# Graph attention kernel: the value product in whole rows of four heads, pair copies alternating between ScalarE and VectorE

## The chip, the core and the metric

The kernel runs on one core of a Trainium2 chip. The metric is the device time of the whole program in microseconds, lower is better. Before the change it is 734.52 us, the median of three runs (733.99 to 735.31).

## The reference, cut to what matters

Sixteen graphs of 512 nodes and 128 features pass through two layers. The first (a norm, a linear map and eight Euler steps of a graph diffusion) is not touched by the change. The second is an attention with four heads of 32 features over each graph, masked by the adjacency:

```python
h = relu(layernorm(x))
qkv = (h @ W).reshape(B, 512, 3, 4, 32).transpose(2, 0, 3, 1, 4)
q, k, v = qkv
scores = einsum('bhid,bhjd->bhij', q, k) / sqrt(32) + mask
attn = softmax(scores, axis=-1)
out = einsum('bhij,bhjd->bhid', attn, v)
x = x + out.transpose(0, 2, 1, 3).reshape(B, 512, 128)
```

All of it is in fp32. The change concerns the last product, `attn` times `v`, and the copies that feed it.

## The kernel before, in words

The kernel has three blocks: a set-up, the diffusion (`ode_block`) and `attention_block` (from line 1107). The second writes q, k, v and the residual of each graph to HBM; the attention reads them back, one graph ("batch") after another.

A batch is 16 score tiles of 128 queries by 512 keys, one for each block of queries and each head. Tile n is block n // 4, head n % 4. Each engine has its own program of a batch, written as a loop over n, and semaphores tie them together. For tile n:

- TensorE (line 1334) multiplies q by k into one of three PSUM banks `ps_s`. It waits until VectorE has emptied the bank, and at n = 0 until the eight q/k loads of this batch have landed.
- VectorE (line 1292) adds the mask, writes the tile to `s_ring` and keeps the row extreme in `low`.
- ScalarE (line 1269) takes the exponential in place and sums it into `lsum`.
- TensorE (line 1321) transposes the tile, four turns later (`LAG = 4`), into half of a two-bank tile `ps_t`. Two tiles are a pair p = 0 to 7; pair p fills `ps_t[p % 2]`, so its transposes wait for the copy of pair p - 2.
- VectorE (line 1286) or ScalarE (line 1260) copies a whole pair, 128 x 1024, to `p_t`. Which engine, is given by `ACT_PAIRS`; where in that engine's order, by `COPY_BEFORE`: pair p is copied before score tile `COPY_BEFORE[p]` of the same batch, and a value of 16 or more means before tile value - 16 of the next batch.

The value product (line 1349) of a batch runs inside the next batch's turns. It has 16 matmuls, k = 0 to 15: row j = k // 4 is a block of 128 keys, hh = k % 4 the head. A head's result takes 32 of the 128 columns of the array and 32 partitions of one bank `ps_o`; the four rows j accumulate. `PV_AT` says behind which turn's transposes how many of them are issued. The first one waits for the last pair copies of both engines, for v and for the bank. Each matmul is fp32 and appears as two instructions in the trace. After turn 13's group ScalarE copies the bank to `o_t` (line 1264), in turn 15 TensorE transposes it back (line 1356), VectorE divides by the sums after score tile 15 (lines 1298 and 1302), and GpSimd adds the residual (line 1246).

SyncE issues all DMAs on one queue, in this order in each batch: v (line 1204, when the value product is done), the residual x1 (line 1206, when GpSimd's add is done), the store of the result (line 1217), then the eight loads of q and k (line 1103), 256 KB each, for the batch behind the one that TensorE has just begun, into the buffers that the last batch has left.

The order of the work is written out by hand in these constants:

```python
ACT_PAIRS = [1, 2, 5, 7]
COPY_BEFORE = [7, 7, 8, 12, 14, 15, 18, 18]
PV_AT = {5: 1, 6: 4, 7: 2, 11: 4, 13: 5}
OCOPY_AT, OT_AT, FIN_AT = 13, 15, 15
```

Batches 1 to 14 are run by a hardware loop whose body holds two batches; batch 0, batch 15 and a last pass without score tiles stand by themselves.

Of the kernel before, what the change touches and what calls it, by code (L numbers as in the profile page):

```python
# [33 lines left out]
HEADS = 4  # L34
HD = D // HEADS
T = N // 128
# [14 lines left out]
def wait(eng, sem, value):  # L51

    if isinstance(value, int) and value <= 0:
        return
    eng.wait_ge(sem, value)  # L55
# [1051 lines left out]
def attention_block(nc, ctx, x1_dram, qk_dram, v_dram, out, keep):  # L1107
# [8 lines left out]
    PAIRS = TILES // 2  # L1116
    RING = 8
    LAG = 4
    ACT_PAIRS = [1, 2, 5, 7]
    DVE_PAIRS = [p for p in range(PAIRS) if p not in ACT_PAIRS]  # L1120

    COPY_BEFORE = [7, 7, 8, 12, 14, 15, 18, 18]


    PV_AT = {5: 1, 6: 4, 7: 2, 11: 4, 13: 5}
    OCOPY_AT, OT_AT, FIN_AT = 13, 15, 15
    assert sum(PV_AT.values()) == HEADS * T
    PV_RANGE = [(sum(PV_AT.get(i, 0) for i in range(n)), sum(PV_AT.get(i, 0) for i in range(n + 1))) for n in range(TILES)]

    S_BANKS = 3  # L1130
# [45 lines left out]
    def copied(p, b):  # L1176

        if p in ACT_PAIRS:
            return t_act, len(ACT_PAIRS) * b + ACT_PAIRS.index(p) + 1
        return t_dve, len(DVE_PAIRS) * b + DVE_PAIRS.index(p) + 1  # L1180

    def pairs_before(n, mine):

        return [(p, COPY_BEFORE[p] // TILES) for p in mine if COPY_BEFORE[p] % TILES == n]

    def copy_pair(eng, p, b, par):
        wait(eng, t_mm, TILES * b + 2 * p + 2)
        if p in (ACT_PAIRS[0], DVE_PAIRS[0]):
            wait(eng, pv_mm, CREDIT + b - 1)
# [62 lines left out]
    def _(act):  # L1252
        def batch(b, par, tiles=TILES):
            first = isinstance(b, int) and b == 0
            for n in range(TILES):
                for p, back in pairs_before(n, ACT_PAIRS):
                    if (first and back) or not (tiles or back):
# [53 lines left out]
    def _(pe):  # L1311
# [13 lines left out]
        def batch(b, par, tiles=TILES):  # L1325
            first = isinstance(b, int) and b == 0
            c, cp = b - 1, 1 - par
            for n in range(TILES):
# [11 lines left out]
                for k in range(*PV_RANGE[n]) if not first else ():  # L1340

                    j, hh = divmod(k, HEADS)
                    if k == 0:
                        for p in (ACT_PAIRS[-1], DVE_PAIRS[-1]):
                            wait(pe, *copied(p, c))
# [19 lines left out]
def graph_block(nc, x, adj, alpha, w, d, fcw, fcb, wqkv, out):  # L1365
    x1_dram = nc.dram_tensor("x1_dram", [B, 128, T, D], F32, kind="Internal").ap()
    qk_dram = nc.dram_tensor("qk_dram", [B, 128, 4, N], F32, kind="Internal").ap()
    v_dram = nc.dram_tensor("v_dram", [B, 128, N], F32, kind="Internal").ap()
    keep = {}
    with ExitStack() as outer:  # L1370
        keep["ident"] = outer.enter_context(nc.sbuf_tensor("ident", [128, 128], F32))
        keep["pH"] = [outer.enter_context(nc.sbuf_tensor(f"pH{k}", [128, T, N], F32R)) for k in range(3)]
        keep["pL"] = [outer.enter_context(nc.sbuf_tensor(f"pL{k}", [128, T, N], F32R)) for k in range(3)]


        assert HEADS == T
        keep["q_st"], keep["k_st"] = keep["pH"][0::2], keep["pL"][0::2]
        for name in ("adj_in", "mask_done", "tail_out"):
            keep[name] = outer.enter_context(nc.semaphore("att_" + name))
        keep["qk_in"] = [outer.enter_context(nc.semaphore(f"qk_in{i}")) for i in range(2)]  # L1380
        with ExitStack() as kept:
            def sb(name, shape, dt=F32R):
                return kept.enter_context(nc.sbuf_tensor(name, shape, dt))
            keep["rH"], keep["rL"] = sb("rH", [128, 3, 3 * D]), sb("rL", [128, 3, 3 * D])
            keep["wH"], keep["wL"] = sb("wH", [128, 3 * D]), sb("wL", [128, 3 * D])
            keep["g"] = sb("g", [128, T, 3 * D], F32)
            ln = FirstNorm(sb, lambda name: kept.enter_context(nc.semaphore(name)))
            with ExitStack() as ctx:
                setup_block(nc, ctx, x, adj, alpha, w, d, fcw, fcb, wqkv, keep, ln)
            with ExitStack() as ctx:  # L1390
                ode_block(nc, ctx, x, adj, x1_dram, qk_dram, v_dram, keep, ln)
        with ExitStack() as ctx:  # L1392
            attention_block(nc, ctx, x1_dram, qk_dram, v_dram, out, keep)
# [20 lines left out]
```

## Time and profile before

| | |
|---|---|
| median of three runs | 734.52 us (733.99 to 735.31) |
| span of the profiled execution | 730.3 us |
| mean granted TensorE clock | 0.982 |
| TensorE matmul busy | 692.7 us, 95% |
| VectorE busy | 486.1 us, 67% |
| ScalarE busy | 400.9 us, 55% |
| GpSimd busy | 121.2 us, 17% |
| value product, line 1349 | 512 instructions of 603 ns, 95.6 us |
| score matmuls, line 1334 | 256 of 495 ns, 126.0 us |
| transposes, line 1321 | 1024 of 275 ns, 155.7 us |
| VectorE pair copy, line 1286 | 64 of 1220 ns |
| ScalarE pair copy, line 1260 | 64 of 1014 ns |

The span is the time between the first and the last instruction of one execution under the profiler; the device time of an execution is longer by what lies around it, 4.2 us between this span and the median. Busy times count overlapping matmuls once, and a matmul's duration includes the part in which the next one already runs. The attention begins at about 413 us; the shares of the whole span mix it with the two blocks before it.

### The profile page before, as it was taken

What the parts mean: (1) busy time and instruction counts of PE and PEld (TensorE: products, weight loads), DVE (VectorE), ACT (ScalarE), POOL (GpSimd) and SP (SyncE); (2) the same over time, 40 slices, a digit from 0 to 9 for tenths busy, and PEclk for the clock granted to TensorE, in tenths of its full rate; (3) what the DMA queues carried; (4) which work ended last, traced back from release to release, by engine and by line L of the source; (5) the groups of instructions that cost most, each with busy time, mean ns of one, the idle gap of its engine ahead of it and who ended that gap; (6) DMA issues with size and microseconds to landing.
All of it is one profiled execution on the core that took longest, in us unless ns stands there. A gap on an engine that the chain in (4) does not pass through costs nothing. (4 is left out here: it accounts for less than half of the span.)

```text
span 730.3 us, 12946 instructions
## 1 busy us (share of the span) xinstructions
PE 692.7 (95%) x3801; PEld 517.3 (71%) x3801; DVE 486.1 (67%) x1272; ACT 400.9 (55%) x860; POOL 121.2 (17%) x100
## 2 busy tenths in 40 slices
PE   7999999998999989999998779999999999999996
PEld 5768987898888978899887655565655555566553
DVE  6753552578337873466346578888888888888883
ACT  3442231233522444222334678888888888888883
POOL 4110343032401233012315000000000000000001
PEclk8999999999999999999998999999999999999999
DMA  3001110311342124400449892666676766766620
GB/s 104 30 0 44 30 44 0 101 31 44 145 167 78 57 80 162 132 15 16 158 175 256 287 213 74 152 139 150 155 158 158 158 148 154 158 157 152 153 57 29
DMA packets 49807, 82.52 MB, mean 113 GB/s; under 512 B 5232, under 2 KB 13808, under 8 KB 49648
## 3 DMA queue, kind: packets, MB, share of 16 engines
q1 hardware_dynamic: 49344, 82.07, 42.5%
q8 instruction: 16, 0.26, 0.2%
q14 instruction: 15, 0.12, 0.1%
q10 hardware_dynamic: 432, 0.07, 0.1%
HBM read 52.76 MB, written 29.36 MB: 112 GB/s over the span
## 5 line engine op out<-in xcount | busy, mean ns | idle before, releaser
L1292 DVE CUSTOM_DVE_ANT_0 s_ring<-ps_s,pL 128x512 f32<-128x512 f32 x256 | 169.0, 688 | 55.0 <-PE ps_s L1334 53.1
L1269 ACT ACTIVATE s_ring<-s_ring,low 128x512 f32<-128x512 f32 x256 | 182.2, 713 | 16.3 <-DVE low L1292 14.8
L1321 PE MATMUL ps_t<-ident,s_ring 128*128 128x128 f32 x1024 | 155.7, 275 | 9.6 <-DVE p_t L1286 9.0
L1321 PEld LDWEIGHTS ps_t<-ident,s_ring 128*128 128x128 f32 x1024 | 127.0, 141 | 31.5 <-DVE p_t L1286 11.6
L1334 PE MATMUL ps_s<-pL,pH 128*128 128x512 f32 x256 | 126.0, 495 | 6.9 <-DMA pL<-qk_dram 3.7
L1334 PEld LDWEIGHTS ps_s<-pL,pH 128*128 128x128 f32 x256 | 48.9, 192 | 75.5 <-DVE low L1292 56.6
L1349 PE MATMUL ps_o<-p_t,v_sb 128*32 128x512 f32 x512 | 95.6, 603 | 1.1 <-ACT p_t L1260 1.1
L1286 DVE COPY p_t<-ps_t 128x1024 f32<-128x1024 f32 x64 | 78.1, 1220 | 0.0
L1260 ACT ACTIVATE p_t<-ps_t 128x1024 f32<-128x1024 f32 x64 | 64.9, 1014 | 21.3 <-PE ps_t L1321 21.3
L1246 POOL TENSOR_TENSOR o_n<-o_n,x 128x512 f32<-128x512 f32 x16 | 20.6, 1285 | 311.4 <-DVE o_n L1302 311.4
L94 PE MATMUL ps_v<-rH,ut_h 128*128 128x384 f32 x192 | 65.1, 339 | 4.6 <-DVE v L927 4.6
L96 PE MATMUL ps_v<-rH,ut_l 128*128 128x384 f32 x192 | 64.5, 336 | 0.0
L95 PE MATMUL ps_v<-rL,ut_h 128*128 128x384 f32 x192 | 64.5, 336 | 0.0
L768 ACT ACTIVATE ut_h<-ps_u 128x512 fp32r<-128x512 f32 x44 | 26.1, 593 | 65.3 <-PE ps_u L96 43.4
L869 DVE TENSOR_TENSOR ut_l<-ps_u,ut_h 128x512 fp32r<-128x512 f32 x44 | 30.3, 688 | 36.2 <-ACT ut_h L768 36.1
L927 DVE TENSOR_TENSOR v<-ps_v,g 128x384 f32<-128x384 f32 x64 | 35.5, 555 | 26.7 <-PE ps_v L96 25.7
L733 POOL TENSOR_TENSOR v_l<-v,v_h 128x512 fp32r<-128x512 f32 x16 | 21.0, 1313 | 176.9 <-ACT v_h L821 176.9
L1269 ACT ACTIVATION_READ_ACCUMULATOR s_ring<-s_ring,low 128x1 f32 x256 | 48.3, 188 | 0.0
L94 PE MATMUL ps_u<-pH,u_h 128*128 128x512 f32 x112 | 45.8, 409 | 0.0
L96 PE MATMUL ps_u<-pH,u_l 128*128 128x512 f32 x112 | 44.3, 395 | 0.0
L95 PE MATMUL ps_u<-pL,u_h 128*128 128x512 f32 x112 | 44.1, 394 | 0.0
L94 PEld LDWEIGHTS ps_v<-rH,ut_h 128*128 128x128 f32 x192 | 36.1, 188 | 6.0 <-DVE v L927 5.6
(201 smaller groups left out, 1087.3 us busy)
## 6 DMA issues: line engine op xcount, KB each, us to landing
pH<-qk_dram SPq DMA_DIRECT2D x64, 256.0 KB, 7.6
pL<-qk_dram SPq DMA_DIRECT2D x64, 256.0 KB, 8.4
qk_dram<-qk SPq DMA_DIRECT2D x12, 512.0 KB, 3.3
x_ln<-in_x SPq DMA_DIRECT2D x16, 256.0 KB, 3.3
x_res<-in_x SPq DMA_DIRECT2D x16, 256.0 KB, 2.6
x_dram<-v SPq DMA_DIRECT2D x16, 256.0 KB, 3.1
v_sb<-v_dram SPq DMA_DIRECT2D x16, 256.0 KB, 2.7
x<-x_dram SPq DMA_DIRECT2D x16, 256.0 KB, 2.9
```

The source lines that it names most:

```text
L94: eng.matmul(psum, lh, rh, start=(first and n == 0), stop=False)
L95: eng.matmul(psum, lh, rl, start=False, stop=False)
L96: mm = eng.matmul(psum, ll, rh, start=False, stop=(last and n == len(pairs) - 1))
L869: dve.tensor_tensor(ut_l[b % 2][:, k, :], u_bank(b, k)[:, :], ut_h[b % 2][:, k, :].bitcast(F32), ALU.subtract).then_inc(ul_done, 1)
L927: dve.tensor_tensor(v[:, t, b, :], ps_v[t % 2][:, 0:3 * D], keep["g"][:, t, :], ALU.add).then_inc(v_add, 1)
L1260: act.activation(dst, src, ACT.Copy).then_inc(t_act, 1)
L1269: act.activation(s_ring[:, n % RING, :], s_ring[:, n % RING, :], ACT.Exp, bias=low[:, n:n + 1], scale=-1.0, accum_out=lsum[par][:, n:n + 1 ...
L1286: dve.tensor_copy(dst, src).then_inc(t_dve, 1)
L1292: dve.tensor_tensor_reduce(s_ring[:, n % RING, :], ps_s[S_BANK[n]][:, :], mask[:, n // HEADS, :], -SCALE, 3.0e38, ALU.add, ALU.min, low[:, ...
L1321: mm = pe.transpose(ps_t[p % 2][:, n % 2, j * 128:(j + 1) * 128], s_ring[:, n % RING, j * 128:(j + 1) * 128], ident[:, :])
L1334: pe.matmul(ps_s[S_BANK[n]][:, :], q_st[par][:, h, it * 128:(it + 1) * 128], k_st[par][:, h, :], start=True, stop=True).then_inc(s_mm, 1)
L1349: mm = pe.matmul(ps_o[cols, :], v_sb[cp][:, j, cols], p_t[cp][:, hh, j, :], start=(j == 0), stop=(j == T - 1), tile_position=(0, HD * hh))
```

## The change

Three tables of the attention are altered and an assertion is tightened. The value product is issued behind turns 5, 9 and 13, four, four and eight matmuls, each a whole number of rows of four heads. Pair 2 passes from ScalarE to VectorE and pair 3 from VectorE to ScalarE, so that odd pairs are ScalarE's and even ones VectorE's. Six of the eight copies are placed at another tile in their engine's order: pair 0 before tile 6 (was 7), pair 2 before 10 (was 8), pair 3 before 13 (was 12), pair 5 before tile 0 of the next batch (was 15), pairs 6 and 7 before its tile 3 (was 2). Nothing else differs.

```diff
-    ACT_PAIRS = [1, 2, 5, 7]
+    ACT_PAIRS = [1, 3, 5, 7]
     DVE_PAIRS = [p for p in range(PAIRS) if p not in ACT_PAIRS]
 
-    COPY_BEFORE = [7, 7, 8, 12, 14, 15, 18, 18]
+    COPY_BEFORE = [6, 7, 10, 13, 14, 16, 19, 19]
 
-    PV_AT = {5: 1, 6: 4, 7: 2, 11: 4, 13: 5}
+    PV_AT = {5: 4, 9: 4, 13: 8}
     OCOPY_AT, OT_AT, FIN_AT = 13, 15, 15
-    assert sum(PV_AT.values()) == HEADS * T
+    assert sum(PV_AT.values()) == HEADS * T and all(n % HEADS == 0 for n in PV_AT.values())
```

## Rows read from the trace of the kernel before

**Rows 1.** Windows, one batch: length, busy us (instructions) by engine, clock, DMA share, GB/s.
```profile
528.70:547.90 19.20, 18.62 (x118) 11.23 (x117) 15.92 (x41) 16.11 (x38) 1.49 (x2) 1.00 0.68 150
```

**Rows 2.** Chain that ended last, in order of time: start us, us, what.
```profile
529.93 0.66 PE ps_t L1321 x4
...
547.93 1.15 DVE p_t L1286
549.12 0.66 PE ps_t L1321 x4
```

**Rows 3.** Timeline of VectorE: start us, us, engine, line, operation.
```profile
527.44 0.68 DVE L1292 CUSTOM_DVE_ANT_0 s_ring<-ps_s,pL 128x512 f32<-128x512 f32 x1
...
546.62 0.69 DVE L1292 CUSTOM_DVE_ANT_0 s_ring<-ps_s,pL 128x512 f32<-128x512 f32 x1
...
547.24 0.69 DVE L1292 CUSTOM_DVE_ANT_0 s_ring<-ps_s,pL 128x512 f32<-128x512 f32 x1
...
547.85 1.22 DVE L1286 COPY p_t<-ps_t 128x1024 f32<-128x1024 f32 x1
```

**Rows 4.** Timeline of TensorE, one batch, turn 0 to the next turn 0.
```profile
526.15 0.48 PE L1334 MATMUL ps_s<-pL,pH 128*128 128x512 f32 x1
...
530.54 0.50 PE L1334 MATMUL ps_s<-pL,pH 128*128 128x512 f32 x1
...
531.40 1.05 PE L1349 MATMUL ps_o<-p_t,v_sb 128*32 128x512 f32 x2
532.38 0.50 PE L1334 MATMUL ps_s<-pL,pH 128*128 128x512 f32 x1
...
533.25 1.06 PE L1349 MATMUL ps_o<-p_t,v_sb 128*32 128x512 f32 x8
...
536.10 0.50 PE L1334 MATMUL ps_s<-pL,pH 128*128 128x512 f32 x1
...
536.79 0.48 PE L1334 MATMUL ps_s<-pL,pH 128*128 128x512 f32 x1
...
537.46 0.48 PE L1334 MATMUL ps_s<-pL,pH 128*128 128x512 f32 x1
...
540.66 0.48 PE L1334 MATMUL ps_s<-pL,pH 128*128 128x512 f32 x1
...
543.34 0.50 PE L1334 MATMUL ps_s<-pL,pH 128*128 128x512 f32 x1
...
545.14 0.48 PE L1334 MATMUL ps_s<-pL,pH 128*128 128x512 f32 x1
```

**Rows 5.** Timeline of ScalarE, the copy of pair 7.
```profile
529.59 1.00 ACT L1260 ACTIVATE p_t<-ps_t 128x1024 f32<-128x1024 f32 x1
```

**Rows 6.** Timeline of SyncE's DMA issues: x1 and last q/k load of two batches.
```profile
509.83 0.35 SPq L1206 DMA_DIRECT2D x<-x_dram  x1
...
515.35 0.65 SPq L1103 DMA_DIRECT2D pL<-qk_dram  x1
...
529.00 0.35 SPq L1206 DMA_DIRECT2D x<-x_dram  x1
...
533.80 0.54 SPq L1103 DMA_DIRECT2D pL<-qk_dram  x1
```

**Rows 7.** DMA issues around 515.35 and 533.80: queue, count, KB, us to landing.
```profile
pL<-qk_dram SPq DMA_DIRECT2D x1, 256.0 KB, 10.3
...
pL<-qk_dram SPq DMA_DIRECT2D x1, 256.0 KB, 10.0
```

**Rows 8.** Timeline of SyncE's DMA issues at the start of the attention.
```profile
419.63 0.34 SPq L1103 DMA_DIRECT2D pL<-qk_dram  x1
420.03 0.63 SPq L1204 DMA_DIRECT2D v_sb<-v_dram  x1
```

**Rows 9.** DMA issues around 419.63 and 420.03, us to landing.
```profile
pL<-qk_dram SPq DMA_DIRECT2D x1, 256.0 KB, 10.4
...
v_sb<-v_dram SPq DMA_DIRECT2D x1, 256.0 KB, 10.9
```

## The prediction

> **What bounds the kernel now.** I went from the page to the windows, then to the chain of waits, then to the timelines of TensorE, VectorE, ScalarE and SyncE over one batch of the attention. The change touches only the attention's loop, whose batches 1 to 15 repeat one pattern. In one such batch TensorE is busy 18.62 of 19.20 us, VectorE 15.92, ScalarE 16.11, at full granted clock (1.00, the 2.4 GHz level) [rows 1]. So no batch can go below about 16.1 us by the busy times of the other two engines, and TensorE is what fills it now. The chain of waits, though, leaves TensorE at one place in each batch: VectorE's pair copy (line 1286), then four transposes that take 0.66 us instead of their usual share, and on [rows 2]. From those transposes to the next ones like them it is 529.93 to 549.12, 19.19 us; the score matmul of turn 0 to that of the next batch is 526.15 to 545.14, 18.99 us [rows 4]. Batches alternate between the two, since the loop's body holds two batches; the mean is 19.09.
>
> I number a batch's turns by the score tile n, 0 to 15. A turn without value product takes 0.69 us right behind a group (536.10 to 536.79) and 0.67 otherwise (536.79 to 537.46) [rows 4]; I take 0.67.
>
> **Part 1, the value product regrouped.** Turn 5 issues one matmul (two instructions) and lasts 530.54 to 532.38 = 1.84; turn 6 issues four (eight instructions) and turn 7 two, and together they last 532.38 to 536.10 = 3.72, 1.86 each [rows 4]. One matmul costs as much as four: the four heads use different 32 columns of the array and run side by side. Every group of up to one of each head costs 1.86 - 0.67 = 1.19 (turn 5: 1.17). Turn 13 issues five, so two on one head's columns, and lasts 540.66 to 543.34 = 2.68, or 2.01 over an empty turn [rows 4]. The trace holds no group of eight between score matmuls. Its lower bound is that same 2.01, since it also has two on each head's columns; its upper bound is two separate groups of four, 2.38. I take 2.03, near the five, because the second row is issued behind the first with no score tile between.
> Before: 1.17 + 1.19 + 1.19 + 1.18 (turn 11, four, as turn 6) + 2.01 = 6.74. After: turns 5, 9, 13 give 1.17 + 1.19 + 2.03 = 4.39. TensorE issues 2.35 us less per batch. Between two bounds for the eight this is 2.0 to 2.37.
>
> **Part 2, which engine copies, and when.** Pair copies are p = 0 to 7; TensorE transposes pair p in turns 2p+4 and 2p+5 (6 and 7 in turns 0 to 3 of the next batch), and the transposes of pair p wait for the copy of pair p-2. Pair 2 goes from ScalarE to VectorE, pair 3 the other way, so each engine keeps four. The edit that costs is pair 6: VectorE did it before score tile 2 of the next batch and now does it before tile 3. Now: score tile 0 starts at 546.62, tile 1 at 547.24, the copy at 547.85, and the transposes of turn 4 start at 549.12 [rows 2, 3]. One VectorE tile takes 547.24 to 547.85 = 0.61 [rows 3]. TensorE reached turn 4 before that (the chain runs through the copy), so nothing hides the 0.61: they start 0.61 later, and everything behind them on TensorE's queue (score tile 5, the value product) waits with them. Lower bound 0, if the copy were not the last to come; upper bound 1.22, if the tile and its successor both fell in front. I take 0.61, the row it is made of.
>
> A rule to weigh. The rows say that VectorE's order, not TensorE's work, sets this stretch, and I take off 0.61 of the 2.35. The Trainium skill, page TensorEngine Tiling (Array Packing), PSUM Bottleneck, warns that packing the array speeds up TensorE but not the copies out of PSUM, which may then become the limit. Without that effect the sum would be 2.35 per batch, with it 1.74.
>
> **The other moves, at nothing, and their cover.** I followed one batch with the starts of the rows, score tile 13 at 0, each operation as soon as its engine and its inputs allow. Turns 14, 15, 0' start at 2.70, 3.37 and 4.48; pair 6 is copied at 7.8, turn 4's transposes start at 9.1, turn 5 at 9.7, turn 13 again at 17.4. (a) Pair 7 on ScalarE goes behind exp 2 instead of before it. Now it starts at 529.59, lasts 1.00, and the first value matmul, which waits for it, starts at 531.40: 0.8 us to spare [rows 4, 5]. ScalarE's step is 0.71 later, TensorE's turn 5 is 0.61 later, so about 0.7 stays. (b) Pair 5 goes behind exp 15 and ends near 6.6 while turn 2's transposes could start at 6.2; this 0.4 us stall, plus a restart, is hidden by the wait for pair 6 at 9.1. If that cover went, it would cost 0.7. (c) Pairs 0 (before tile 6), 2 (VectorE, before tile 10, done near 16.1 against a need at 17.1) and 3 (ScalarE, before exp 13, done 0.4 before turn 14 needs it) fall in VectorE's and ScalarE's free time. If (c) lost its 0.4, the stall would be the excess. (d) No DMA is added or moved, but SyncE's waits are: the x1 load, the store and the eight q/k loads follow the add on GpSimd, which follows score tile 15, at the same distance.
>
> **Part 3, the q/k loads.** They must land before score tile 0 of the next batch. The x1 load is issued at 529.00, the last q/k load at 533.80 and lands 10.0 later, at 543.8; the deadline is 545.14: 1.34 to spare. In the batch before: 515.35 + 10.3 = 525.65 against 526.15, 0.50 to spare [rows 4, 6, 7]. A late score tile 0 is also absorbed until VectorE would start it: it starts 0.69 after TensorE's at the earliest, and now starts at 546.62 and 527.44, 0.79 and 0.60 beyond that [rows 3, 4]. The spare time is 2.1 and 1.1. A batch 1.74 shorter leaves 0.4 and -0.6. Since the stall also delays the next chain of loads, half of the 0.6 or so stays, in every other batch: about 0.2 per pair after the scatter of the landings, 1.5 us in all. Bounds: 0 and 7 x 0.6 = 4.
>
> **Sum.** Batches 1 to 15: 15 x (2.35 - 0.61) = 26.1 us off, 1.5 back, 24.6. Batch 0 has no value product and the next one waits for its loads; the last product (all 16 matmuls without score tiles between) stays one block. From the span of the profiled execution, 730.3, to 705.7. The median of the runs, 734.5, lies 4.2 above that span, the time around it: 734.5 - 24.6 = **709.9**, say 710.
>
> **Rivals.**
> A. The copy of pair 6 costs nothing, all 2.35 arrive: 15 x 2.35 = 35 less, 700. For: VectorE idles elsewhere. Against: the chain goes through this very copy in every batch [rows 2]. Chance 0.08.
> B. The q/k loads become the bound. For: the spare time is used up by the sum itself. Each us that the landing comes later costs about 0.5 per batch (a load issued after one batch is needed two starts later). One us more gives 717, two 724. Against: the load of v is now issued while q/k packets are still in flight, but it need not slow them: at the start, v issued at 420.03 landed after 10.9, at 430.9, behind q/k issued at 419.63 that took 10.4, to 430.0 [rows 8, 9]. Chance 0.17.
> C. Slower than before. The copy of pair 7 on ScalarE comes so late that the first value matmul waits in TensorE's queue, with score tile 6 and all behind it. Its place is turn 5; it decides from 0.7 (the spare time) + 1.74 = 2.4 us of lateness on; at 3 us, 15 x 0.6 = 9 more, 743. For: pair 5 and pair 7 both moved behind one more exp. Against: ScalarE has 3 us free per batch [rows 1], and the exps before it have no other late input. Chance 0.04.
> D. The change does not shorten the groups: a row of four takes longer after other work than turn 6 shows. Then no change, 734. Turn 6 is measured, so 0.03.
> My forecast keeps 0.68.
>
> **Numbers.** A measurement of this kernel can tell about 0.2%, 1.5 us. Range 703 to 719: below, the eight and the loads at nothing and part of A; above, the lighter half of B. Faster 0.93, same 0.03, slower 0.04.
>
> **What would show it.** Right: value product in groups of 8, 8 and 16 instructions, turns 5 and 9 near 1.86, turn 13 near 2.70; transposes of turn 4 released by VectorE's copy, with 0.6 us more wait than now; period near 17.4; score tile 0 now waiting for a DMA by up to 0.9 us in some batches. Wrong: score tile 0 waiting over 1 us in all batches (B); first value matmul released by ScalarE (C); turn 4 without a wait (A); turn 2 or turn 14 on the chain (my free moves).

## The result and the profile after

The changed kernel takes 712.58 us (707.21 to 714.85, four runs) against 734.91 of the kernel before on the same chips: ratio 0.9686, 95% interval 0.9655 to 0.9717, 22.3 us less. A second set of six runs gave 712.27 and 0.9706 (0.9675 to 0.9738). The forecast was 710.0, range 703 to 719.

The profiled execution took 707.21 with a span of 705.4, so 1.8 us lie around the span; it was the quickest of its four. The prediction had put 4.2 there for the kernel before. Every run on record of either kernel is 1.8 or 1.9 longer than its span, so the span of 730.3 belongs to an execution of about 732.1, quicker than all the runs of its median, and the other 2.4 are scatter. The forecast doesn't suffer, since the same amount is taken off both. Medians are compared with medians below, and periods with periods.

The page of the changed kernel, engines and costliest groups:

```profile
PE 655.7 (93%) x3801; PEld 511.2 (72%) x3801; DVE 488.7 (69%) x1272; ACT 398.8 (57%) x860; POOL 121.2 (17%) x100
...
L1321 PE MATMUL ps_t<-ident,s_ring 128*128 128x128 f32 x1024 | 155.4, 275 | 17.4 <-DVE p_t L1286 11.9
...
L1334 PE MATMUL ps_s<-pL,pH 128*128 128x512 f32 x256 | 125.1, 491 | 10.6 <-DMA pL<-qk_dram 7.1
...
L1349 PE MATMUL ps_o<-p_t,v_sb 128*32 128x512 f32 x512 | 64.5, 601 | 1.1 <-ACT p_t L1260 1.1
```

The value product has the same 512 instructions of the same length (601 ns, 603 before) but keeps TensorE busy 64.5 us where it was 95.6: more of them run side by side. TensorE is busy 37 us less in all, and the runs got only 22 us faster. The third column says where part of the rest went: the score matmuls wait 7.1 us for a DMA, eight times, where before it was 3.7, once, in batch 1.

The timeline of TensorE, from one batch's turn 0 to the next, and the later turns 0 (columns: start us, us, instruction, and in brackets the idle time before it with what ended it):

```profile
499.75 0.50 PE L1334 MATMUL ps_s<-pL,pH 128*128 128x512 f32 x1 [1.02 <-DMA pL<-qk_dram]
...
502.45 0.48 PE L1334 MATMUL ps_s<-pL,pH 128*128 128x512 f32 x1
503.75 0.65 PE L1321 MATMUL ps_t<-ident,s_ring 128*128 128x128 f32 x4 [0.82 <-DVE p_t L1286]
504.16 0.48 PE L1334 MATMUL ps_s<-pL,pH 128*128 128x512 f32 x1
...
505.01 1.07 PE L1349 MATMUL ps_o<-p_t,v_sb 128*32 128x512 f32 x8
506.00 0.50 PE L1334 MATMUL ps_s<-pL,pH 128*128 128x512 f32 x1
...
511.92 0.48 PE L1334 MATMUL ps_s<-pL,pH 128*128 128x512 f32 x1
...
512.76 1.92 PE L1349 MATMUL ps_o<-p_t,v_sb 128*32 128x512 f32 x16
514.62 0.50 PE L1334 MATMUL ps_s<-pL,pH 128*128 128x512 f32 x1
...
516.48 0.50 PE L1334 MATMUL ps_s<-pL,pH 128*128 128x512 f32 x1
...
533.49 0.49 PE L1334 MATMUL ps_s<-pL,pH 128*128 128x512 f32 x1
```

Against [rows 4]: turn 5 has four matmuls and lasts 504.16 to 506.00 = 1.84, as with one. Turn 13 has eight and lasts 511.92 to 514.62 = 2.70, against 2.68 with five. Turn 4's transposes still wait for VectorE's copy, 0.82 us here, but the score matmul behind them starts 0.41 later (503.75 to 504.16), where it was 0.61 before ([rows 2, 4], 529.93 to 530.54).

The DMA wait of 1.02 is not in every batch. From the turn 0 behind it to the next, which does not wait, it is 16.73 us (499.75 to 516.48); then 17.01, and the next 18.64 (533.49 to 552.13) with a wait of 1.16. Over 13 periods (first turn 0 446.52, last 674.25) the mean is 17.52, before 19.08. A second profiled execution of the changed kernel, 712.22 us and so near the median, has 17.64 over the same 13 (448.27 to 677.58). The chain of waits says what that long batch hung on: SyncE's last q/k issue, and its landing.

```profile
540.20 0.81 SPq L1103
...
541.10 0.65 SPq L1103
...
541.84 10.17 DMA pL<-qk_dram
...
552.13 0.49 PE ps_s L1334
```

That load is no slower than its like in [rows 6, 7]. From the x1 load to the landing of the last q/k load the changed kernel takes 15.2 us on average over 13 batches, and the kernel before 15.1. What changed is when it is needed.

### The profile page after: what moved, and what is told of

It is laid out like the page before. It is cut to its first block, busy times and chain, and to the rows that moved or that the text cites. A ratio compares the mean times of both kernels' runs of the same rounds, so it can differ in the third digit from the quotient of the medians.

```text
span 705.4 us, 12953 instructions
## 1 busy us (share of the span) xinstructions
PE 655.7 (93%) x3801; PEld 511.2 (72%) x3801; DVE 488.7 (69%) x1272; ACT 398.8 (57%) x860; POOL 121.2 (17%) x100
## 4 chain that ended last, share of the span: by engine, by line
PE 34%; DMA 11%; DVE 6%; issue 5%; SPq 4%; POOL 1%; ACT 1%; POOLq 0%; DVEq 0%; ACTq 0%
DMA pL<-qk_dram 10%; PE ps_t L1321 7%; PE ps_s L1334 5%; PE ps_o L1349 4%; SPq L1103 3%; PE ps_z L1015 2%; PE ps_z L1011 2%; PE ps_z L1010 2%; PE ps_u L94 2%; PE ps_u L96 1%; PE ps_u L95 1%; PE ps_v L94 1%; PE ps_v L96 1%; PE ps_v L95 1%; DVE p_t L1286 1%
## 5 line engine op out<-in xcount | busy, mean ns | idle before, releaser
L1321 PE MATMUL ps_t<-ident,s_ring 128*128 128x128 f32 x1024 | 155.4, 275 | 17.4 <-DVE p_t L1286 11.9
L1349 PE MATMUL ps_o<-p_t,v_sb 128*32 128x512 f32 x512 | 64.5, 601 | 1.1 <-ACT p_t L1260 1.1
L95 PE MATMUL ps_v<-rL,ut_h 128*128 128x384 f32 x192 | 64.5, 336 | 0.0
L768 ACT ACTIVATE ut_h<-ps_u 128x512 fp32r<-128x512 f32 x44 | 26.1, 594 | 65.4 <-PE ps_u L96 43.4
```

What stands on the lines that cost most here:

```text
L95: eng.matmul(psum, lh, rl, start=False, stop=False)
L1321: mm = pe.transpose(ps_t[p % 2][:, n % 2, j * 128:(j + 1) * 128], s_ring[:, n % RING, j * 128:(j + 1) * 128], ident[:, :])
L1349: mm = pe.matmul(ps_o[cols, :], v_sb[cp][:, j, cols], p_t[cp][:, hh, j, :], start=(j == 0), stop=(j == T - 1), tile_position=(0, HD * hh))
```

## Experiments

All were compared with the kernel before on the same chip. There were three of them, on which the kernel before took 734.34 (A), 735.48 (B) and 734.65 (C); where two runs come from different chips, a difference of medians is good to about 1 us, and the ratios are the better guide. Medians in us:

| run | chip | median (runs) | ratio, 95% interval |
|---|---|---|---|
| changed kernel, two sets | -, A | 712.58 (4), 712.27 (6) | 0.9686 (0.9655 to 0.9717), 0.9706 (0.9675 to 0.9738) |
| tables only | B | 741.93 (6) | 1.0097 (1.0069 to 1.0125) |
| groups only | B | 717.53 (6) | 0.9754 (0.9724 to 0.9783) |
| changed, early q/k | B | 707.74 (6) | 0.9615 (0.9588 to 0.9642) |
| changed, late q/k | A | 715.49 (5) | 0.9741 (0.9715 to 0.9767) |
| before, early q/k | A | 734.30 (12) | 1.0000 (0.9978 to 1.0023) |
| before, late q/k | A | 735.24 (12) | 1.0014 (0.9996 to 1.0032) |
| changed, pair 6 first | B | 717.15 (5) | 0.9761 (0.9734 to 0.9789) |
| the same, early q/k | C | 717.19 (6) | 0.9754 (0.9722 to 0.9787) |
| groups, old tables, pair 0 moved | C | 709.62 (6) | 0.9662 (0.9637 to 0.9686) |
| the same, early q/k | C | 705.72 (6) | 0.9605 (0.9575 to 0.9636) |
| early q/k, pairs 5 to 7 at old places | C | 698.16 (6) | 0.9507 (0.9476 to 0.9538) |

**The two halves of the change.** First the tables without the groups:

```diff
-    PV_AT = {5: 4, 9: 4, 13: 8}
+    PV_AT = {5: 1, 6: 4, 7: 2, 11: 4, 13: 5}
```

> The new copy tables with the old groups of the value product (1, 4, 2, 4, 5). Theory: pair 6's copy one score tile later on VectorE puts 0.61 us per batch on the chain, 15 x 0.61 = 9 us slower than before, ratio 1.012. Rival: the tables are free by themselves, within 0.2% of before.

Measured 6.5 us slower than before. The timeline of TensorE in that run:

```profile
508.83 0.48 PE L1334 MATMUL ps_s<-pL,pH 128*128 128x512 f32 x1
...
512.13 0.47 PE L1334 MATMUL ps_s<-pL,pH 128*128 128x512 f32 x1
513.41 0.66 PE L1321 MATMUL ps_t<-ident,s_ring 128*128 128x128 f32 x4 [0.81 <-DVE p_t L1286]
513.83 0.48 PE L1334 MATMUL ps_s<-pL,pH 128*128 128x512 f32 x1
...
528.42 0.48 PE L1334 MATMUL ps_s<-pL,pH 128*128 128x512 f32 x1
```

The direction is the theory's, its size a third smaller. Turn 4's transposes start 4.58 after turn 0 where it was 3.98 in the same half of the loop (545.14 to 549.12, [rows 2, 4]), so the 0.61 is there. But the next score matmul follows after 0.42 instead of 0.61. It waits for tile 2 to leave its PSUM bank, and VectorE now takes tile 2 ahead of the copy. Before, VectorE's tile 2 ended at 549.66, and score tile 5 began 0.07 later:

```profile
548.98 0.68 DVE L1292 CUSTOM_DVE_ANT_0 s_ring<-ps_s,pL 128x512 f32<-128x512 f32 x1
```

The batches take 19.37 and 19.59, the mean is 19.48 against 19.08: 0.40 per batch, 15 x 0.40 = 6.0.

Then the groups without the tables:

```diff
-    ACT_PAIRS = [1, 3, 5, 7]
+    ACT_PAIRS = [1, 2, 5, 7]
-    COPY_BEFORE = [6, 7, 10, 13, 14, 16, 19, 19]
+    COPY_BEFORE = [7, 7, 8, 12, 14, 15, 18, 18]
```

> The new groups (4, 4, 8) with the old tables. Theory: TensorE's 2.35 us per batch come off, but the q/k loads then end last in most batches (period 17.1 where the engines alone would give 16.8), so 15 x 2.0 = 30 off, near 705, and less than the changed kernel's 712.6 by 4 to 8. Rival: the old tables collide with the new groups (pair 2 on ScalarE before tile 8, pair 3 on VectorE before tile 12), and it is slower than the changed kernel, 715 or more.

The rival was right: 717.5, 5 us slower than the changed kernel (3.5 to 5 by the ratios). The timelines of TensorE and of VectorE in two batches of it show a second wait:

```profile
529.21 0.47 PE L1334 MATMUL ps_s<-pL,pH 128*128 128x512 f32 x1
530.51 0.66 PE L1321 MATMUL ps_t<-ident,s_ring 128*128 128x128 f32 x4 [0.83 <-DVE p_t L1286]
```

```profile
546.54 0.69 DVE L1292 CUSTOM_DVE_ANT_0 s_ring<-ps_s,pL 128x512 f32<-128x512 f32 x1 [0.86 <-PE ps_s L1334]
...
547.16 1.22 DVE L1286 COPY p_t<-ps_t 128x1024 f32<-128x1024 f32 x1
```

Turn 8's transposes wait 0.83 us for pair 0. VectorE sat idle for 0.86 with that copy next but one in its order: score tile 6 stood in front, and tile 6 comes only after turn 5's value product. Before, turns 6 and 7 carried value product too and hid this. So the collision is real, but in this run it shows at pair 0, not at pairs 2 and 3 as the rival had it: turn 12's transposes start 0.32 behind their score matmul here, without a wait. That one entry, by itself, on top of the groups:

```diff
     ACT_PAIRS = [1, 2, 5, 7]
-    COPY_BEFORE = [7, 7, 8, 12, 14, 15, 18, 18]
+    COPY_BEFORE = [6, 7, 8, 12, 14, 15, 18, 18]
```

> New groups, old tables, with only pair 0 moved from tile 7 to tile 6. In the run with all old tables (717.5) turn 8's transposes waited 0.8 us for VectorE's copy of pair 0, which stood behind score tile 6, itself behind the four matmuls of turn 5. Theory: this one entry is what the new groups need of the tables; the wait goes, 1.1 us per batch less where the q/k loads allow it: 708 to 712. Rival: several entries are needed, it stays above 715.

709.6: 7.9 us less than with all old tables by the medians, 6.8 by the ratios. That the 3 us to the changed kernel are a gain is not shown, since the intervals overlap. The groups need pair 0 moved; the other changes to the tables, taken together and with the loads where they are, bring nothing measurable on top. The trace has turn 8 without a wait, and another one in its place:

```profile
516.69 0.47 PE L1334 MATMUL ps_s<-pL,pH 128*128 128x512 f32 x1
517.30 0.65 PE L1321 MATMUL ps_t<-ident,s_ring 128*128 128x128 f32 x4
```

This is turn 12, with 0.61 where 0.32 is usual, and so in every batch. The late copy of pair 0 had hidden it; what it is shows below, where the rival's pair 2 comes back.

**Is it the q/k loads?** SyncE issues the eight loads ahead of x1 and the store, in the changed kernel and in the one before:

```diff
         def batch(b, par):
...
-            if not last:
-                load(b + 1, 1 - par)
-            if not first:
-                store(b - 1, 1 - par)
+            if not (const and b == B - 1):
+                load_q(b + 1, 1 - par)
+            if not (const and b == 0):
+                load_x(b, par)
+            if not (const and b < 2):
+                store(b - 2, par)
+            if not (const and b == B - 1):
+                load_v(b + 1, 1 - par)
```

> The changed kernel with SyncE's order altered: the eight q/k loads go ahead of the residual's load and of the store, so they are issued some 4 us earlier in each batch. Theory: the changed kernel's unprofiled runs lose to late q/k loads; with the loads early score tile 0 waits for no DMA, the period is 17.3 to 17.4, the time 703 to 706, and the runs lie within 3 us of each other. Rival: the 4 to 5 us between the changed kernel's median and its fastest run come from elsewhere, and it stays at 711 to 713 with the same scatter.

> The kernel before with the q/k loads ahead of the residual's load and the store. Theory: with a period of 19.1 the loads land 1.1 to 2.1 us before they are needed, so earlier loads bring nothing: within 0.3% of before. Rival: earlier loads help by something else than the wait at score tile 0 (a shorter first batch, less contention), and bring the 5 us that they brought in the changed kernel.

The functions `load_q`, `load_x` and `load_v` are the old `load` in three pieces; they and the first and last batches, written out by themselves, are left out here.

And the same loads held back, in both:

```diff
-                wait(sp, s_mm, CREDIT + TILES * (b - 1))
+                wait(sp, s_mm, CREDIT + TILES * (b - 1) + 6)
```

> The changed kernel with the q/k loads held back until score tile 5 of the batch is done, some 0.6 to 0.9 us later than now. Theory: the loads end last, and each us of lateness costs about half a us per batch: 14 x 0.5 x 0.75 = 5 us more than the changed kernel, near 718. Rival: their landing is hidden, 712 to 713.

> The kernel before with the same hold until score tile 5. Theory: the spare time of 1.1 to 2.1 us covers it, within 0.3% of before. Rival: 5 us slower, as in the changed kernel.

> The changed kernel itself, as the control for the three others of this group. 711 to 713.

Early loads take 4.5 to 4.8 us off the changed kernel (5.2 to 6.7 by the ratios, whose intervals don't touch) and nothing off the kernel before; late loads add 3.2 to the changed one, and to the kernel before 0.9, inside its interval. The 3.2 alone would not be proof, since the intervals of the two ratios overlap; the waits below bear it out. The signs fit the theory; early landed at 707.7, above the 703 to 706 expected, and late cost less than the 5 worked out. With early loads the waits list shows no DMA wait of TensorE from batch 2 on, and turn 0 comes at

```profile
502.37 0.48 PE L1349 MATMUL ps_s<-pL,pH 128*128 128x512 f32 x1
...
519.61 0.48 PE L1349 MATMUL ps_s<-pL,pH 128*128 128x512 f32 x1
...
536.66 0.48 PE L1349 MATMUL ps_s<-pL,pH 128*128 128x512 f32 x1
```

17.24 and 17.05, mean 17.15, a little under the 17.3 to 17.4 expected (the longer program moves the line numbers by 15). That is 0.37 under the changed kernel's 17.52 and 0.50 under the 17.64 of its second profiled execution; over 13 periods 4.9 and 6.5 us, about what the medians say. With late loads every turn 0 from batch 2 on waits, and the mean period is 17.83:

```profile
PE ps_s L1334 <- DMA pL<-qk_dram: 12.8, 14, 1.1
```

The theory said more than that: that the changed kernel's runs scatter because of the loads. This is mostly not so. With early loads the runs still lie within 4.2 us, the changed kernel's within 5.7 in its second set and 7.6 in its first. And of the 5.0 us between the spans of its two profiled executions (705.4 and 710.4) only 1.6 lie in the 13 periods; 2.5 lie in batches 0 and 1, where the granted clock of the stretch 413 to 450 was 0.91 in the quicker and 0.86 in the slower one, and 1.7 behind the last turn 0. The rest, -0.7, is the start of the attention.

**Pair 6 back to its place.** In the changed kernel, and again with early loads:

```diff
-    COPY_BEFORE = [6, 7, 10, 13, 14, 16, 19, 19]
+    COPY_BEFORE = [6, 7, 10, 13, 14, 16, 18, 19]
```

> The changed kernel with pair 6 copied before score tile 2 again, pair 7 left. Theory: VectorE's chain is 0.61 us shorter per batch, but the q/k loads then hold score tile 0, so that a third to a half of 15 x 0.61 arrives: 3 to 5 us less than the changed kernel, near 708. Rival: the copy isn't the limit, no difference to the changed kernel (712).

Both theories missed: 717.2, 5 us slower than the changed kernel (4.0 to 5.5 by the ratios). The waits, then ScalarE's timeline in one batch:

```profile
PE ps_o L1349 <- ACT p_t L1260: 13.9, 14, 1.0
```

```profile
540.76 0.71 ACT L1269 ACTIVATE s_ring<-s_ring,low 128x512 f32<-128x512 f32 x1
...
542.39 0.72 ACT L1269 ACTIVATE s_ring<-s_ring,low 128x512 f32<-128x512 f32 x1 [0.83 <-DVE low L1292]
...
543.11 1.00 ACT L1260 ACTIVATE p_t<-ps_t 128x1024 f32<-128x1024 f32 x1
```

The first value matmul waits 1.0 us for ScalarE in each batch, the wait of rival C at its place. VectorE copies pair 6 and reaches tile 2 later; exp 2 waits for tile 2; the copy of pair 7 stands behind exp 2. Pair 6 behind tile 2 and pair 7 behind exp 2 belong together.

> Early q/k loads and pair 6 before score tile 2, pair 7 still behind exp 2. In the run without early loads (717.2) the copy of pair 6 held score tile 2, exp 2 behind it, and pair 7 behind that, and the first value matmul waited 1.0 us for ScalarE in each batch. Theory: that wait is the cause and has nothing to do with the loads, so it stays: near 711 to 714, slower than early loads alone (707.7) by 3 to 6. Rival: the late loads were the cause; with early loads it is 0.4 x 14 = 6 less than 707.7, near 702.

717.19, and the wait is there again, 1.0 in each of 14 batches, so it has nothing to do with the loads. The time is above the 711 to 714 expected: the periods average 17.82, which is the 17.15 of early loads alone, less 0.40 for pair 6, plus the wait of 1.0 (17.75).

**A version that beats both.** Early loads and the new table for pairs 0 to 4, but pairs 5, 6 and 7 all at their old places; beside it, early loads on the old tables with pair 0 moved.

```diff
-    COPY_BEFORE = [6, 7, 10, 13, 14, 16, 19, 19]
+    COPY_BEFORE = [6, 7, 10, 13, 14, 15, 18, 18]
```

> The same with early q/k loads. Theory: VectorE's chain is 0.4 us per batch shorter than with pair 6 behind tile 2, and no load cuts it off: period 16.75, 707.7 - 14 x 0.4 = 702. Rival: another stall takes the place, 706 or more.

> Early q/k loads, the new tables for pairs 0 to 4, the old places for pairs 5, 6 and 7 (before tiles 15, 2, 2). Theory: who copies pairs 2 and 3 does not matter, so the same as the kernel with the old tables and pair 0 moved, 702, within 2 us. Rival: pair 2 on VectorE before tile 10 or pair 3 on ScalarE before exp 13 costs or gains over 3 us against it.

The kernel with pair 0 moved and early loads took 705.7, not the theory's 702, and near the rival's 706: another stall did take the place. The one with the new tables for pairs 0 to 4 took 698.16, 4.9% faster than the kernel before and 7.5 us from the other, so its rival was right too, and the tables of pairs 2 and 3 do matter. TensorE's turns 0, first in the 698 us version, then in the other with turn 12 of its batch:

```profile
499.87 0.48 PE L1349 MATMUL ps_s<-pL,pH 128*128 128x512 f32 x1
...
516.73 0.48 PE L1349 MATMUL ps_s<-pL,pH 128*128 128x512 f32 x1
...
533.41 0.48 PE L1349 MATMUL ps_s<-pL,pH 128*128 128x512 f32 x1
```

```profile
503.37 0.48 PE L1349 MATMUL ps_s<-pL,pH 128*128 128x512 f32 x1
...
515.05 0.47 PE L1349 MATMUL ps_s<-pL,pH 128*128 128x512 f32 x1
515.67 0.65 PE L1336 MATMUL ps_t<-ident,s_ring 128*128 128x128 f32 x4
...
537.61 0.48 PE L1349 MATMUL ps_s<-pL,pH 128*128 128x512 f32 x1
```

The periods are 16.77 and 17.12 on average. In the second, turn 12's transposes start 0.62 after their score matmul, where 0.32 is usual (0.61 to 0.63 in all batches, as without early loads), since exp 8 comes late: with old tables ScalarE copies pair 1 and pair 2 with one exp between. Its timeline:

```profile
512.23 1.00 ACT L1275 ACTIVATE p_t<-ps_t 128x1024 f32<-128x1024 f32 x1
...
513.13 0.71 ACT L1284 ACTIVATE s_ring<-s_ring,low 128x512 f32<-128x512 f32 x1
...
513.84 1.01 ACT L1275 ACTIVATE p_t<-ps_t 128x1024 f32<-128x1024 f32 x1
...
514.74 0.71 ACT L1284 ACTIVATE s_ring<-s_ring,low 128x512 f32<-128x512 f32 x1
```

The 0.35 between the periods makes 5 us of the 7.4 between the two spans; 1.8 more lie in batches 0 and 1 (17.82 and 18.28 against 17.14 and 17.12), and why is open. Pairs 2 and 3 changed engine and place together, so the runs don't say which of these counts; the trace points to pair 2 leaving ScalarE. The best version without early loads was not tried, nor was each of pairs 5 to 7 alone.

## Why the prediction was right, and where it was off

**Part 1, 2.35 per batch: right.** Groups of 1.84 and 2.70 as costed; the eight cost 2.03 over an empty turn, the value taken. In the 698 us version, with VectorE's old order around turn 4 and no DMA wait, the period is 16.77; the sum of part 1 alone is 19.09 - 2.35 = 16.74.

**Part 2, pair 6 at 0.61: place and sign right, size off.** It measured 0.40. The transposes did start 0.61 later, as the step had it. But it counted only the tile in front of the copy, and missed that taking tile 2 earlier frees the bank for which score tile 5 waits right behind the stall. With 0.40 the period is 19.08 - 2.35 + 0.40 = 17.13; 17.15 was measured with early loads.

**The rule on PSUM copies: half right.** The warning of the Trainium skill, page TensorEngine Tiling (Array Packing), PSUM Bottleneck, holds here through order, not yet through load, as far as the runs show: the same 16 tiles and four copies on VectorE allow 16.77 or 17.15, by the place of the pair copies. Four tables were tried with the new groups and early loads, and their periods (16.77 to 17.82) all lie above the 16.1 to which VectorE and ScalarE are busy [rows 1]. The load is close behind, though: in the 698 us version, between 450 and 550 us, TensorE is busy 96.5 us, ScalarE 94.5 and VectorE 93.1.

**The other moves at nothing: right in the sum, wrong as a picture.** No stall of (a), (b) or (c) reached the chain of the changed kernel; (b)'s wait of turn 2 shows as 0.3 to 0.4 us, covered. But pair 0's move was costed at nothing, and is worth 7 to 8 us once the groups stand (717.5 to 709.6). The change was costed from the old order, in which turn 8 does not stall; I never asked what the groups do without the tables. And the cover of (a) is 0.5 to 0.6, not 0.7. In the batch shown above, whose first value matmul starts at 505.01, ScalarE's copy of pair 7 ends at 504.39:

```profile
503.39 1.00 ACT L1260 ACTIVATE p_t<-ps_t 128x1024 f32<-128x1024 f32 x1
```

With pair 6 a tile earlier this copy ends 0.95 later, counted from turn 0, and TensorE's turn 5 starts 0.41 earlier (both with early loads), which is more than the cover and leaves the wait of 1.0.

**Part 3, q/k loads at 1.5 us: the mechanism right, the term mis-sized.** They cost 4.9 us over 13 periods in one profiled execution and 6.5 in the other, 4.5 to 4.8 by the medians. All of these lie above the term's own upper bound of 4. The landing stayed as it was (15.2 against 15.1). Two numbers moved the need forward: the batch is 1.95 shorter, not 1.74; and of a late turn 0 only 0.4 to 0.6 us is absorbed, not 0.79 and 0.60. With early loads turn 4's transposes start 4.4 to 4.6 after turn 0, and after a wait at turn 0, 4.0 after it. That is rival B in its direction, without the later landing that it needed, and at 3 to 5 us over my sum, where one us of later landing would have cost 7.

**Sum by measured terms:** 15 x (2.35 - 0.40) = 29.3 less, 4.9 to 6.5 back: 22.8 to 24.4, where I had 26.1 - 1.5 = 24.6. Two errors of 3 to 5 us cancelled: that the sum came this close is luck. The medians moved 22.3, the spans of the two profiled executions 24.9. Rival A did not happen, nor D. C's mechanism was found in two experiments, at 1.0 us, not at the 2.4 that it needed.

## What to carry to other kernels

Regrouping work on one engine moves the moment at which others get their input, so the order tables that surround it are part of the same change: here the groups alone gave 18 us, the tables alone lost 6.5, together they gave 22, the groups with one entry of the tables 25, and another choice of tables with earlier loads 36. When a loop gets shorter, list every transfer with its spare time against the new period, and count only as much absorption as the next wait in line shows. Ask of each copy which instruction of the same engine waits behind it, and who waits for that one.

## What the runs showed that I had not expected

A queue position can cost through a third engine: VectorE's copy one tile earlier made TensorE wait 1.0 us for ScalarE in each batch. The q/k loads make batches alternate rather than lag evenly: a batch of 16.7 to 16.9 without a wait is followed, mostly, by one of 18.1 to 18.6 with one. Held back, the loads landed 16.0 us after the x1 load in place of 15.2, every batch from the second on waited, and most took 17.7 to 18.1; the 0.8 us cost 3.2 us in all by the medians, less than the half a us per batch and us that I had used (5.6).
